# First attention: the last four units of a slot are scaled on ScalarE and added on VectorE

## The chip, the cores and the metric

One core of one Trainium2 chip runs the whole kernel in one launch. The metric is device time in microseconds (us). The kernel before took 5300.93 us, the median of three runs (5298.13 to 5308.7). Five engines work beside each other, each through its own instruction queue in order: TensorE (PE, with its weight loads as PEld), VectorE (DVE), ScalarE (ACT), GpSimd (POOL) and SyncE (SP). They wait for each other through semaphores.

## What is computed

The reference is a graph network of two layers on 6250 nodes with 256 features, each layer an attention over 106250 edges followed by a mixture of experts:

```python
x = x + L0_gnn(layernorm(x), edges)     # attention 0: 4 heads of 64
x = x + L0_ffn(layernorm(x))            # 6 experts, the best 2 of each node
x = x + L1_gnn(layernorm(x), edges)     # attention 1: 1 head of 256
x = x + L1_ffn(layernorm(x))            # 8 experts, all of them, weighted

# attention, per edge (src -> dst) and head
e = leaky_relu(a_src[src] + a_dst[dst])
m = segment_max(e, dst)
e = exp(e - m[dst])
out[n] = sum over edges into n of e * h[src] / sum over edges into n of e
```

The edges come sorted by destination. The change touches attention 0 alone.

## The kernel before, in words

**Tiles, units and slots.** The 6250 nodes are 50 tiles of 125. The edges of a tile are cut into units of 256 (`UE`), 464 units in all, in the order of the tiles, so that some nine units in a row belong to one tile. Eight units (`U`) make a slot, and there are 58 slots. `attention(l, acc, sc)` writes the program of each engine as a function `slot(i, r, t)`. The first and last slots are unrolled, the others are a hardware loop of three slots per turn, with three buffers (`RING`).

**A running maximum.** The softmax is made in one pass. `acc` holds, for each node of each tile, the sum so far of the weighted rows and of the weights: 4 heads x 65 columns (`W`, 64 features and the weight's sum). When a unit raises the maximum, what is in `acc` must be multiplied by a factor first. The factors of a slot are `c1`, made on ScalarE in L867 (an Exp of `delta`). The merge of one unit is `acc = acc * c1 + sum`, with the sum in a PSUM bank, per head because each head has its own factor.

**The stations of a slot i**, by engine:
- SP loads the unit's edge records (`pack`, L658) and its destination rows (`drow`, L671).
- POOL gathers the source rows from HBM into `G` by indirect DMA (L687), 16 for a slot, two per unit. Before the two of unit u it waits until TensorE has summed unit u of slot i - 3, whose rows lie in the buffer.
- TensorE in iteration i: two transposes for slot i - 1 once its rows have landed (L734, L735), the sums of units 4 to 7 of slot i - 3 (L720, with `spread` 0 and 1, L705, ahead of unit 7), two transposes (L746, L747), the sums of units 0 and 1 of slot i - 2, the small product `V` (L757), `spread` 2 and 3, the sums of units 2 and 3, and the product `Xe` (L770). Four banks are shared: unit u and unit u + 4 use the same one, so each sum waits for the merge four units before.
- ScalarE in iteration i: a copy `LT` (L825), then `place` (L791, two operations) and `hit` (L803) for each of four quarters of the slot, the Exp `w` of slot i - 2's weights (L833), a copy `RS_hi` (L840), eight copies `rhsA` (L850), and the factors `c1` (L867).
- VectorE in iteration i: `dloc` (L970), reductions and small operations that end in `te` (L996) and `SEL` (L1001), then the weights are multiplied into `G` in four quarters, `scale(0)` to `scale(3)` (L940, 128x1024 each), with the merges between them, the scan of the maxima (L1014 to L1061, among them `gone`, L1028, which waits for `V`), and the one-hot matrices of slot i, `incidence(0)` to `(3)` (L957).

**The merges' places.** On VectorE `scale(0)`, merges of units 4 and 5 of slot i - 3, L1007, `scale(1)`, merges of units 6 and 7, then the scan; the merges of units 0 to 3 of slot i - 2 stand at the iteration's end, between the `incidence` steps. The function is `merge(k, u)`, and it has two ways:

```python
if u in own:
    v.wait_ge(S(p + "lowered"), scaled_acc(k, i, u))
    ins = nc.vector.tensor_tensor(at, at, sum_bank(u)[0:TN, 0:HW], ALU.add)          # L918
else:
    for h in range(H):
        ins = nc.vector.scalar_tensor_tensor(at, at, c1[...], sum_bank(u)[...], ALU.mult, ALU.add)   # L925
ins.then_inc(S(p + "acc"), 1)
```

`own` holds the units that are not in `FUSED[l]`. In the kernel before it is empty in both layers, so all merges go by L925, and ScalarE's counterpart `lower(k, u)` (from L805 on) returns without an instruction wherever it is called.

Of the kernel before, what the change touches and what calls it, by code (L numbers as in the profile page):

```python
# [36 lines left out]
U = 8  # L37
# [18 lines left out]
assert UE == 1 << LOG_UE and (SU + LAG) % RING == 0 and RING * V % MR == 0 and SU * U <= KU * P and (NG + 1) % 2 == 0 and EP * EC == E  # L56

HEADS = (4, 1)
FUSED = ((0, 1, 2, 3, 4, 5, 6, 7), (0, 1, 2, 3, 4, 5, 6, 7))
SLOPES = (0.2, 0.01)  # L60
EXPERTS = (6, 8)
XT = 256
# [5 lines left out]
def build(nc, a, out):  # L68
    ctx = ExitStack()
    with ctx:  # L70
# [6 lines left out]
        def S(name):  # L77

            if name not in sems:
                sems[name] = nc.alloc_semaphore(name=f"{name}_{stage[0]}")  # L80
            return sems[name]
# [8 lines left out]
        def after(eng, name, count):  # L90

            if not isinstance(count, int) or count > 0:
                eng.wait_ge(S(name), count)
# [53 lines left out]
        def late(i, k):  # L147

            return not isinstance(i, int) or i >= k
# [395 lines left out]
        def attention(l, acc, sc):  # L545
# [9 lines left out]
            K3 = C + 1  # L555
            own = [u for u in range(U) if u not in FUSED[l]]
            NA = len(own)
# [64 lines left out]
            def has(i, lag):  # L622

                return not isinstance(i, int) or lag <= i < SU + lag
# [13 lines left out]
            with nc.Block() as block:  # L638
# [137 lines left out]
                def _(act):  # L776
                    tile_regs = [[act.alloc_register(f"{p}atile{k}_{u}") for u in range(U)] for k in range(RING)]

                    def slot(i, r, t):
# [3 lines left out]
                        def place(v_):  # L783

                            if not one:
                                return
                            act.wait_ge(S(p + "spread"), i * V - V + (v_ + 1))
                            if v_ >= 2 or late(i, 2):
                                after(act, p + "MT", i * V - V + (v_ - 1))
                            for k in range(2):  # L790
                                ins = nc.scalar.activation(mt_d[:, v_ % 2, k * C:(k + 1) * C, :],  # L791
                                                           bank[2 + v_ % 2][0:TN, k * UE:(k + 1) * UE].rearrange("p (e c) -> p c e", c=C), ACT.Abs,
                                                           bias=unode[0:TN, bass.ds(i * U - U + (2 * v_ + k), 1)])
                            ins.then_inc(S(p + "mt_abs"), 1)

                        def hit(v_):

                            if not one:
                                return
                            act.wait_ge(S(p + "mt_abs"), i * V - V + (v_ + 1))  # L800
                            if late(i, 3 if v_ < 2 else 2):
                                after(act, p + "Xe", i - 2 if v_ < 2 else i - 1)
                            nc.scalar.activation(MT[:, turn(r, 1, v_), :, :], mt_d[:, v_ % 2, :, :], ACT.Relu, bias=ones[0:TN, 0:1], scale=-1.0).then_inc(S(p + "MT"), 1)  # L803

                        def lower(k, u):  # L805

                            if u not in own or not has(i, k):
                                return
                            rk = (r - k) % RING
                            j = act.snap(tile_regs[rk][u], min_val=0, max_val=NT - 1)  # L810
                            if u == own[0]:
                                act.wait_ge(S(p + "c1"), i - k + 1)
                            if u or late(i, k + 1):
                                after(act, p + "acc", i * U - k * U + u)
                            for h in range(H):
                                at = acc[:, bass.ds(j * HW + h * W, W)]
                                ins = nc.scalar.activation(at, at, ACT.Copy, scale=c1[:, rk, u, h:h + 1])
                            ins.then_inc(S(p + "lowered"), 1)

                        if one:  # L820
                            act.reg_load(tile_regs[r1], unit_j[0:1, bass.ds(i * U - U, U)])
                            act.wait_ge(S(p + "rowT"), i)
                            if late(i, 2):
                                after(act, p + "SEL", i - 1)
                            nc.scalar.copy(LT[:, :], rowT_ps[:, P:2 * P]).then_inc(S(p + "LT"), 1)  # L825
                        place(0)
                        lower(3, U - 2)
                        hit(0)
                        if two:

                            act.wait_ge(S(p + "te"), i - 1)
                            to = wt[:, r2, :, :] if l == 1 else G[:, r2, :, :].rearrange("p q (h w) -> p q h w", h=H)[:, :, :, DH]
                            nc.scalar.activation(to, te[:, :, :], ACT.Exp).then_inc(S(p + "w"), 1)  # L833
                        lower(3, U - 1)
                        place(1)
                        if one:
                            act.wait_ge(S(p + "selT"), i)
# [4 lines left out]
                        if one:  # L842
# [7 lines left out]
                                ins = nc.scalar.copy(rhs[:, u, :, 0:KT, :].rearrange("p s k h -> p s (k h)"),  # L850
                                                     tab[:, bass.ds(j, 1), :, :, :].rearrange("p o s k h -> p (o s) (k h)"))
                            ins.then_inc(S(p + "ad_in"), 1)
                        lower(2, 0)
                        place(2)
                        lower(2, 1)
                        hit(2)
                        place(3)
                        lower(2, 2)
                        hit(3)
                        lower(2, 3)  # L860
                        lower(2, 4)
                        lower(2, 5)
                        if one:
                            act.wait_ge(S(p + "delta"), i)
                            if late(i, RING + 1):
                                after(act, p + "acc", i * U - U * RING)
                            nc.scalar.activation(c1[:, r1, :, :], delta[:, :, :], ACT.Exp).then_inc(S(p + "c1"), 1)  # L867
                    run(act, slot)

                @block.vector  # L870
# [1074 lines left out]
```

## Time and profile before

| | us |
|---|---|
| median of three runs | 5300.93 |
| the profiled execution | 5292.68 |
| its span, first to last instruction | 5290.9 |
| granted TensorE clock over the span, share of full speed | 0.778 |
| PE busy | 3470.2 (66%) |
| VectorE busy | 2702.5 (51%) |
| POOL busy | 2200.9 (42%) |
| ScalarE busy | 1540.1 (29%) |
| attention 0, from its first factors to its last (L867, 58 of them) | 253.5 to 1647.5 |

The span is 1.8 us shorter than the profiled execution's own time. The busy shares are means over stages with different limits, so the stage that the change touches has to be read by itself. Two labels of the releasers are leftovers: semaphore numbers are used again from stage to stage, and in attention 0 a wait of L791 that is put down to `DMA X<-in_x` is a wait for TensorE's `spread` (L705), and a wait of L825 put down to `DMA ubase<-unit_base` is one for TensorE's transpose L735. The code has no other waits there of that kind.

### The profile page before, as it was taken

How to read it: one execution, taken by the hardware profiler on the slowest of the kernel's cores; microseconds unless marked ns; L12 is line 12 of the kernel's file. 1: busy time of each engine (PE TensorE's matmuls, PEld its weight loads, DVE VectorE, ACT ScalarE, POOL GpSimd, SP SyncE). 2: the span in 40 equal slices, each digit the busy share in tenths (PEclk: the TensorE clock that was granted, in tenths of full speed). 3: DMA queues.
4: the chain of work that ended last, by engine and by line, in shares of the span. 5: the costliest groups of instructions: out<-in, count | busy, mean ns of one | idle time of the engine just before them, and what ended most of it. 6: DMA issues, size and time to landing. Idle time of an engine off the chain costs nothing. (4 is left out here: it accounts for less than half of the span.)

```text
span 5290.9 us, 78218 instructions
## 1 busy us (share of the span) xinstructions
PE 3470.2 (66%) x16240; PEld 2639.6 (50%) x16241; DVE 2702.5 (51%) x8451; ACT 1540.1 (29%) x4325; POOL 2200.9 (42%) x2095
## 2 busy tenths in 40 slices
PE   5166566666656788753545555445555799999999
PEld 3144344444434677632333333333333688888887
DVE  7377777777777855463444444444444531122221
ACT  2133323332322123311222222222222233333333
POOL 0377777777771033285655555555554000000000
PEclk9576777676776589966766666677677899999999
DMA  3233333333344144443333333333335100000000
GB/s 100 72 90 87 87 89 86 89 88 87 89 85 84 33 144 156 130 105 86 83 73 74 71 75 79 71 75 76 73 78 65 51 7 6 6 6 6 6 6 6
DMA packets 382420, 367.81 MB, mean 70 GB/s; under 512 B 249324, under 2 KB 309388, under 8 KB 382242
## 3 DMA queue, kind: packets, MB, share of 16 engines
q0 software_dynamic: 107072, 272.84, 20.9%
q1 hardware_dynamic: 272774, 92.39, 7.3%
q10 hardware_dynamic: 2396, 0.84, 0.1%
q14 instruction: 144, 1.18, 0.1%
q8 instruction: 34, 0.56, 0.0%
HBM read 324.13 MB, written 41.59 MB: 69 GB/s over the span
## 5 line engine op out<-in xcount | busy, mean ns | idle before, releaser
L687 POOL DMA_INDIRECT g_G<-rows,g_pack x1856 | 1946.6, 1049 | 1336.8 <-DMA g_pack<-edge_pack 621.3
L720 PE MATMUL bank<-g_G,g_MB 128*125 128x260 f32 x1856 | 704.3, 542 | 214.6 <-DVE acc L925 86.2
L720 PE MATMUL bank<-g_G,g_M 128*125 128x257 f32 x1856 | 672.0, 524 | 157.4 <-issue 101.2
L791 ACT ACTIVATE g_mt_d<-bank,unode 125x256 bf16<-125x256 f32 x928 | 384.5, 464 | 1196.0 <-DMA n_yg<-expert_out,pos_i 451.9
L925 DVE SCALAR_TENSOR_TENSOR acc<-acc,g_c,bank 125x65 f32 (+1 forms) x2320 | 621.5, 317 | 113.2 <-issue 55.9
L720 PEld LDWEIGHTS bank<-g_G,g_MB 128*125 128x125 f32 x1856 | 473.9, 269 | 401.1 <-issue 172.8
L720 PEld LDWEIGHTS bank<-g_G,g_M 128*125 128x125 f32 x1856 | 470.0, 266 | 312.0 <-issue 177.0
L1365 DVE SCALAR_TENSOR_TENSOR X<-bank,e_cw,X 125x256 f32 (+1 forms) x400 | 175.2, 480 | 845.1 <-PE bank L1191 845.1
L1261 ACT ACTIVATE e_h<-bank,e_bi_c,e_sc_c 128x250 f32<-128x250 f32 x800 | 403.6, 555 | 559.6 <-PE bank L1182 421.6
L770 PE MATMUL bank<-g_rhs,g_MT 125*128 125x24 bf16 (+1 forms) x1856 | 65.3, 171 | 491.1 <-issue 461.7
L1191 PE MATMUL bank<-e_w,e_h 128*125 128x256 f32 x1600 | 377.8, 379 | 3.1 <-ACT e_h L1261 3.1
L1182 PE MATMUL bank<-e_h,e_w 128*128 128x250 f32 x1600 | 378.4, 379 | 1.2 <-ACT e_h L1261 1.2
L1173 PE MATMUL bank<-e_xnT,e_w 128*128 128x250 f32 x1600 | 372.4, 375 | 0.0
L803 ACT ACTIVATE g_MT<-g_mt_d,ones 125x512 bf16<-125x512 bf16 x464 | 335.5, 723 | 14.1
L770 PEld LDWEIGHTS bank<-g_rhs,g_MT 125*128 125x128 bf16 x1856 | 58.1, 100 | 560.5 <-issue 548.0
L940 DVE TENSOR_TENSOR g_G<-g_G 128x1024 f32<-128x1024 f32 x232 | 283.3, 1222 | 97.2 <-ACT g_G L833 74.8
L1191 PEld LDWEIGHTS bank<-e_w,e_h 128*125 128x125 f32 x1600 | 299.1, 187 | 47.3 <-ACT e_h L1261 3.9
L1173 PEld LDWEIGHTS bank<-e_xnT,e_w 128*128 128x128 f32 x1600 | 304.0, 190 | 36.4 <-issue 0.7
L1182 PEld LDWEIGHTS bank<-e_h,e_w 128*128 128x128 f32 x1600 | 297.1, 191 | 43.3 <-issue 8.0
L957 DVE TENSOR_TENSOR g_MB<-iota_b,g_dloc 128x500 f32<-128x500 bf16 (+1 forms) x464 | 302.3, 674 | 0.1
L825 ACT COPY g_LT<-bank 64x128 f32<-64x128 f32 (+1 forms) x116 | 29.7, 256 | 847.7 <-DMA ubase<-unit_base 436.0
L1785 POOL DMA_INDIRECT x_xg<-expert_in,ids x108 | 111.1, 1029 | 298.5 <-PE bank L1801 200.0
(302 smaller groups left out, 4162.1 us busy)
## 6 DMA issues: line engine op xcount, KB each, us to landing
g_G<-rows,g_pack POOLq DMA_INDIRECT x1856
acc<-in_edge_attr SPq DMA_DIRECT2D x50, 531.2 KB
g_pack<-edge_pack SPq DMA_DIRECT2D x928, 2.0 KB
g_drow<-edge_dst SPq DMA_DIRECT2D x928, 1.0 KB
expert_out<-x_y SPq DMA_DIRECT2D x54, 256.0 KB
g_qe<-edge_q SPq DMA_DIRECT2D x464, 1.0 KB
rows<-acc SPq DMA_DIRECT2D x25, 253.9 KB
rows<-n_T SPq DMA_DIRECT2D x25, 251.0 KB
```

Of the source, the lines that this page charges most:

```text
L687: nc.gpsimd.indirect_dma_start(G[:, r, q, :], None, rows_d[l], bass.IndirectOffsetOnAxis(ap=pack[:, r, q, 0:1], axis=0)).then_inc(S(p + f" ...
L720: mm_ = nc.tensor.matmul(sum_bank(u)[0:TN, 0:HW], left, G[:, rk, q, :], start=(c == 0), stop=(c == C - 1))
L791: ins = nc.scalar.activation(mt_d[:, v_ % 2, k * C:(k + 1) * C, :], bank[2 + v_ % 2][0:TN, k * UE:(k + 1) * UE].rearrange("p (e c) -> p c ...
L803: nc.scalar.activation(MT[:, turn(r, 1, v_), :, :], mt_d[:, v_ % 2, :, :], ACT.Relu, bias=ones[0:TN, 0:1], scale=-1.0).then_inc(S(p + "MT" ...
L925: ins = nc.vector.scalar_tensor_tensor(at, at, c1[:, rk, u, h:h + 1], sum_bank(u)[0:TN, h * W:(h + 1) * W], ALU.mult, ALU.add)
L940: ins = nc.vector.tensor_tensor(g[:, :, 0:DH], g[:, :, 0:DH], g[:, :, DH:W].broadcast_to([P, CP * H, DH]), ALU.mult)
L957: nc.vector.tensor_tensor(MB[:, r, at, :], iota_b[:, 0:TN].unsqueeze(1).broadcast_to([P, CP, TN]), dloc[:, r, at, 0:1].broadcast_to([P, CP ...
L1173: mm = nc.tensor.matmul(bank[m][:, 0:GN], w1[:, e, k, m * P:(m + 1) * P], xnT[:, r, k, :], start=(k == 0), stop=(k == 1))
L1182: mm = nc.tensor.matmul(bank[2 + m][:, 0:GN], w2[:, e, k, m * P:(m + 1) * P], h1[:, k, :], start=(k == 0), stop=(k == 1))
L1191: mm = nc.tensor.matmul(bank[4 + u][0:TN, 0:D], h2[:, e % 2, k, u * TN:(u + 1) * TN], w3[:, e, k, :], start=(k == 0), stop=(k == 1))
L1261: ins = nc.scalar.activation((h1 if q == 0 else h2[:, e % 2, :, :])[:, m, :], bank[2 * q + m][:, 0:GN], ACT.Relu, bias=bi_c[:, q, m, e:e + ...
L1365: ins = nc.vector.scalar_tensor_tensor(xt, bank[4 + u][0:TN, 0:D], cw[:, r, u, e:e + 1], xt, ALU.mult, ALU.add)
```

## The change

`FUSED` of layer 0 now holds units 0 to 3 alone, so `own` is units 4 to 7. For each of these 232 units ScalarE multiplies the unit's accumulator by the factors, four activations of 125x65 (`lower`, L817, one per head), and VectorE adds the PSUM sum with one `tensor_tensor` of 125x260 (L918) in place of four operations of 125x65. `lower(3, u)` waits for `c1` of that slot (unit 4 only) and for the merge before (`acc`); `merge` waits for `lowered`. The calls of `lower` get new places in ScalarE's order. Those that are taken out wrote no instruction.

```diff
-FUSED = ((0, 1, 2, 3, 4, 5, 6, 7), (0, 1, 2, 3, 4, 5, 6, 7))
+FUSED = (tuple(range(4)), tuple(range(8)))
...
                             nc.scalar.copy(LT[:, :], rowT_ps[:, P:2 * P]).then_inc(S(p + "LT"), 1)
+                        lower(3, 4)
                         place(0)
-                        lower(3, U - 2)
                         hit(0)
                         if two:
...
                             nc.scalar.activation(to, te[:, :, :], ACT.Exp).then_inc(S(p + "w"), 1)
-                        lower(3, U - 1)
+                        lower(3, 5)
                         place(1)
...
                             ins.then_inc(S(p + "ad_in"), 1)
-                        lower(2, 0)
+                        lower(3, 6)
+                        lower(3, 7)
                         place(2)
-                        lower(2, 1)
                         hit(2)
                         place(3)
-                        lower(2, 2)
                         hit(3)
-                        lower(2, 3)
-                        lower(2, 4)
-                        lower(2, 5)
                         if one:
                             act.wait_ge(S(p + "delta"), i)
```

`lower`, as it stands in the code:

```python
if u == own[0]:
    act.wait_ge(S(p + "c1"), i - k + 1)
if u or late(i, k + 1):
    after(act, p + "acc", i * U - k * U + u)
for h in range(H):
    at = acc[:, bass.ds(j * HW + h * W, W)]
    ins = nc.scalar.activation(at, at, ACT.Copy, scale=c1[:, rk, u, h:h + 1])
ins.then_inc(S(p + "lowered"), 1)
```

VectorE's order is not changed. Attention 1 and the other stages are not touched.

## Rows read from the trace of the kernel before

**Rows 1.** The page: busy tenths of VectorE and POOL, slices of 132 us.
```profile
DVE  7377777777777855463444444444444531122221
...
POOL 0377777777771033285655555555554000000000
```

**Rows 2.** Busy time in attention 0: start, length, engines, clock, DMA.
```profile
300.00:1500.00 1200.00, 737.57 (x3488) 496.49 (x3489) 915.86 (x3151) 364.87 (x1166) 868.93 (x777) 0.71 0.35 88
```

**Rows 3.** Groups of L687, POOL's only line, 300 to 1500 us.
```profile
L687 POOL DMA_INDIRECT g_G<-rows,g_pack x777 | 869.9, 1120 | 331.4 <-issue 215.7 <-remote 61.7 <-PE bank L720 53.4
```

**Rows 4.** Timeline of a long stall: start, us, engine, line, what [idle before].
```profile
603.10 0.74 PE L705 MATMUL bank<-g_drow,ones_bf 2*125 2x512 bf16 x2
...
609.85 0.95 POOL L687 DMA_INDIRECT g_G<-rows,g_pack  x1 [0.30 <-issue]
612.67 0.23 DVE L1028 TENSOR_SCALAR g_gone<-bank 125x64 f32<-125x64 f32 x1 [7.81 <-remote]
612.81 0.84 ACT L791 ACTIVATE g_mt_d<-bank,unode 125x256 bf16<-125x256 f32 x2 [13.66 <-DMA X<-in_x]
...
613.58 0.95 POOL L687 DMA_INDIRECT g_G<-rows,g_pack  x1 [2.78 <-remote]
```

**Rows 5.** Timeline of one ordinary slot, from PE's transposes on.
```profile
1031.61 0.27 PE L735 MATMUL bank<-ident,g_dloc 128*64 128x128 f32 x1
...
1034.76 0.64 PE L705 MATMUL bank<-g_drow,ones_bf 2*125 2x512 bf16 x2
...
1038.69 0.94 POOL L687 DMA_INDIRECT g_G<-rows,g_pack  x1 [0.30 <-issue]
1038.99 0.26 ACT L825 COPY g_LT<-bank 64x128 f32<-64x128 f32 x1 [9.16 <-DMA ubase<-unit_base]
...
1040.84 0.84 ACT L791 ACTIVATE g_mt_d<-bank,unode 125x256 bf16<-125x256 f32 x2 [1.59 <-DMA X<-in_x]
...
1041.30 0.95 POOL L687 DMA_INDIRECT g_G<-rows,g_pack  x1 [1.67 <-remote]
...
1042.34 0.30 ACT L833 ACTIVATE g_G<-g_te 128x64 f32<-128x64 f32 x1
...
1043.81 0.85 DVE L925 SCALAR_TENSOR_TENSOR acc<-acc,g_c,bank 125x65 f32 x4
...
1044.72 3.83 PE L720 MATMUL bank<-g_G,g_MB 128*125 128x260 f32 x8 [3.50 <-issue]
...
1048.04 0.86 DVE L925 SCALAR_TENSOR_TENSOR acc<-acc,g_c,bank 125x65 f32 x4 [0.24 <-DVE acc L925]
...
1049.30 1.22 DVE L940 TENSOR_TENSOR g_G<-g_G 128x1024 f32<-128x1024 f32 x1
1049.39 1.94 POOL L687 DMA_INDIRECT g_G<-rows,g_pack  x1 [0.30 <-issue]
...
1051.49 0.23 DVE L1028 TENSOR_SCALAR g_gone<-bank 125x64 f32<-125x64 f32 x1 [0.97 <-remote]
```

**Rows 6.** Timeline of the slot after it, at its start.
```profile
1061.66 0.86 DVE L925 SCALAR_TENSOR_TENSOR acc<-acc,g_c,bank 125x65 f32 x4 [2.45 <-PE bank L720]
...
1061.89 0.26 ACT L825 COPY g_LT<-bank 64x128 f32<-64x128 f32 x1 [7.07 <-DMA ubase<-unit_base]
1062.27 0.84 ACT L791 ACTIVATE g_mt_d<-bank,unode 125x256 bf16<-125x256 f32 x2
...
1065.25 0.32 ACT L833 ACTIVATE g_G<-g_te 128x64 f32<-128x64 f32 x1 [1.39 <-issue]
```

**Rows 7.** Groups by shape, 150 to 1700 us: busy us, mean ns of one.
```profile
L925 DVE SCALAR_TENSOR_TENSOR acc<-acc,g_c,bank 125x65 f32 x1856 | 399.5, 277 | 66.8 <-issue 38.6 <-DVE acc L925 20.4 <-PE bank L720 7.2
...
L791 ACT ACTIVATE g_mt_d<-bank,unode 125x256 bf16<-125x256 f32 x464 | 192.3, 464 | 472.9 <-DMA X<-in_x 216.9 <-PE bank L705 194.2 <-issue 59.2
L803 ACT ACTIVATE g_MT<-g_mt_d,ones 125x512 bf16<-125x512 bf16 x232 | 168.0, 724 | 7.1
...
L1033 DVE TENSOR_TENSOR g_SB<-g_SB,bank 125x64 f32<-125x64 f32 x58 | 15.4, 266 | 2.0
```

## The prediction, made before the changed kernel ran

> **What bounds the kernel now.** The chain that ended last lies in the dense experts, so it says nothing of attention 0. I went from the slices to the stage. In the first 13 slices VectorE is busy seven tenths of the time and POOL seven to eight [rows 1]; neither is full, so a slot is paced by a chain with waits. In the 1200 us from 300 on POOL issued 777 gathers, 16 a slot, hence 48.6 slots of 24.7 us [rows 2, 3].
>
> POOL's slot: a gather lasts 1.120 us in the mean and the least step to the next is 0.30 us [rows 3, 5], so 16 x 1.42 = 22.7 us. The rest of its idle time is (331.4 - 777 x 0.30) / 48.6 = 2.0 us a slot, one pause. It comes where POOL needs TensorE to have summed unit 4 of the slot three back. That sum is not late in the records: TensorE's L705, which stands behind it in the queue, is recorded as done at 1035.40, yet ScalarE's L791, which waits for L705, starts at 1040.84 and POOL goes on at 1041.30 [rows 5]. POOL's last gather before had ended at 1039.63, 1.2 us before ScalarE's start. The long stall shows the same more plainly: L705 is recorded as done at 603.84, POOL gathers until 610.80, and at 612.67 and 612.81 VectorE and ScalarE start after 7.8 and 13.7 us of nothing [rows 4]. So as I read it, TensorE's signals are held back while POOL issues gathers without a break, and come through one to two us after POOL stops. POOL stops because it needs one of them. The slot is then POOL's 22.7 us plus its pause, and VectorE, ScalarE and TensorE have slack.
>
> **The change, part by part.**
>
> (1) The add. L1033, a two-operand operation with one operand in PSUM, takes 266 ns for 64 columns, and L940 takes 1.22 us for 1024 [rows 5, 7], 1.0 ns a column; 260 columns give 0.46 us. The four L925 took 0.85 [rows 5]. VectorE saves 0.39 x 232 = 90 us of busy time (at least 0.85 - 0.46, at most 0.85 - 0.27 = 0.58 each, were the add as short as L1033). All of it lies beside POOL's work, so it is worth nothing by itself.
>
> (2) The scaling. The nearest rows are L791 with 256 columns, 464 ns and 0.38 apart (two end after 0.84), and L803 with 512 columns, 724 ns [rows 5, 7]: also 1.0 ns a column. An activation of 65 columns is then 0.27 us, one starts 0.19 after the other, and a unit's four take 0.27 + 3 x 0.19 = 0.84 us. Bounds: below, 4 x 65 columns at 1.0 ns, 0.26 us; above, two L791 pairs, 1.7 us. I take 0.84, which is read off the same engine. ScalarE gets 195 us more work and is busy 365 of 1200 us now [rows 2], so load is no matter; order is.
>
> (3) The hand-over. Unit 5 can be scaled only after unit 4 is merged, 6 after 5, 7 after 6. For each step I take the 0.24 us that VectorE needs between two merges [rows 5], and 0.15 for the way back (between nothing and 0.3). Counted from the end of L833 (1042.64): scale(0) to 1.25, merge 4 to 1.65, lower 5 to 2.7. Behind lower 5 on ScalarE wait L791, L840, L803 and the eight L850, which now end about 2.5 us later, at 5.2; lower 6 ends at 6.1, merge 6 at 6.7, lower 7 at 7.75, merge 7 at 8.4. Before, merge 7 ended at 1048.90, which is 6.3. **Plus 2.1 us** for merge 7 and what is queued behind it on VectorE: the scan, scale(2), scale(3), the factors, four merges, the one-hot matrices. At L1028 VectorE waited 0.97 us for a signal of TensorE [rows 5]; that wait is used up first, so the tail is 1.2 us late.
>
> (4) Lower 4 stands between L825 and L791. Where L825 comes early (here 1039.25 against 1040.84 [rows 5]) it is hidden. Where L825 itself was held (1062.15 against 1062.27 [rows 6]) L791, L803, L833 and scale(0) start 0.8 us later. Of the 50 slots in the middle, 25 are of the second kind.
>
> (5) TensorE. Unit 0's sum starts as soon as merge 4 has freed the bank (1044.72 after 1044.66 [rows 5]), so 0.39 us earlier, and unit 1's after it. Unit 2 needs merge 6, at 6.7 against a start at 7.3; unit 3 needs merge 7, at 8.4 against about 9.2. Nothing of it is late.
>
> (6) Is the lateness absorbed? From one L833 to the next it is 22.9 us in the pair of slots shown, with 0.97 + 2.45 us of waits for TensorE in it [rows 5, 6]: 19.5 us of work. The turn of the loop adds about 2 us in one slot of three, mean 20.2. Plus 2.1, plus 0.8 where L825 was held: 23.1, under 24.7. TensorE's unit 4 is summed 4 us before POOL asks, and 1 to 2 us of that go. POOL's pace stays.
>
> (7) What can move POOL: gathers last 0.94 us at least but 1.12 in the mean [rows 3, 5]; the long ones lie under L940, as 1.94 us at 1049.39 under L940 from 1049.30 [rows 5]. A gather that starts under such an operation with both operands in SBUF ends after it. Scale(0) now starts after a gather's start and costs none. Shifted by 0.8 us in 29 slots of 58 it meets the next gather's start, for up to 1.0 us each, 0 to +29 us; scale(1) and (2), shifted too, may lose stretch, some -20. I take +8 us. The skill says otherwise: the Trainium skill's page SBUF — State Buffer, section Who interferes with whom, infers that such an operation doesn't stall the writing of descriptors, since it takes the read side alone; the row of 1.94 us speaks against that, and by the page this term would be 0 and the sum 5300.9. For the new add I take nothing, as its second operand is in PSUM.
>
> **Sum:** the profiled execution 5292.7 + 8 = 5300.7. The median of runs is 8.3 above that execution, so 5309.
>
> **The rivals.**
>
> A, above: POOL's pace holds. Its own range is 5290 to 5335.
>
> B, slower: ScalarE and VectorE handing the accumulator to and fro become the pace. For it: 23.1 us is near 24.7, and waits that are held may not be absorbed. Against: 3.4 us of waits in the pair shown. Its place is lower 5 to merge 7. Each of the four lowers on that chain would have to cost 0.4 us more than 0.84, or signals be held in one more slot of three. At the upper bound, 1.7 us, the slot is 23.1 + 3.4 = 26.5, +1.8 x 58 = +104 us; halfway +50. So 5350 to 5405. The Trainium skill's page ScalarE: Activation LUTs, section Rules for kernel authors, sends multiplications to VectorE; with that page's figures for an activation with a pointer operand my estimate is 1.06 us a unit, which alone would make the chain 24.0 and leave A standing.
>
> C, faster: what paces the slot is merge 4, units 0 and 1, V, L705, and the signals are late by TensorE's own work. Then 0.39 us of each slot goes, less 0.8 in the held half where scale(0) is late: between -23 and 0, so 5278. If VectorE's shorter tail counts as well, 5255. Against: 603.84 to 612.81 [rows 4].
>
> D, slower: the new add stretches gathers as L940 does. A gather's start falls under 0.46 us in 0.46 of 1.42 cases and then costs 0.23 in the mean, +17 us; at most 0.46 x 232 = +107. So 5326.
>
> **How the numbers follow.** About 0.2% (11 us) is what a measurement of this kernel can tell from no change. A has 0.50 (same 0.32, slower 0.13, faster 0.05), B 0.26 (all but 0.01 slower), C 0.18 (0.17 faster), D 0.06 (slower). Faster 0.22, same 0.34, slower 0.44. The forecast is A's 5309. The range takes in most of C and B: 5270 to 5390.
>
> **What would show it.** In the changed profile: L918 232 times at 0.4 to 0.5 us; L817 928 times, four in 0.8 to 1.1 us; VectorE idle before L918 of units 5, 6 and 7, ended by ScalarE; L1028 without its wait; POOL's mean gather 1.10 to 1.16 us and its idle beyond 0.30 still near 2.0 us a slot. B is right if POOL's idle time grows by 0.9 us a slot or more while its gathers stay at 1.12. C is right if that idle shrinks. D is right if gathers are long under L918. I am wrong on the whole if the 58 factors (L867) span less than 1380 us or more than 1420, against 1394 now.

## The result, and the profile after

The changed kernel takes 5351.73 us (median of 6 runs, 5338.78 to 5367.4), the kernel before on the same chip 5304.82 (6 runs, 5278.14 to 5314.89). The ratio is 1.0092, interval [1.0071, 1.0113]: **slower by 47 us**. The time lies in the range (5270 to 5390) but not where the forecast put it (5309): it is in rival B's band, 5350 to 5405.

Where it went, by the first and last start of the factors in each attention (L867, now L863) and by the borders of the stages:

| stage, us | before | after |
|---|---|---|
| attention 0, 58 factors | 1394 | 1444 |
| between the two attentions' gathers | 827 | 820 |
| attention 1, 58 factors | 1610 | 1620 |
| dense experts (their first TensorE instruction) to the end | 1159 | 1157 |

The profiled execution has a span of 5342.2 us, 51.3 more than before, and attention 0 has 50 of it. Only this stage has to be explained. The changed kernel's lines past `merge` are four lower than before: L921 is L925, L936 is L940, L953 is L957, L1024 is L1028; the new add is L914, the scaling L817.

The page of the changed kernel, busy tenths of VectorE and POOL in slices of 134 us, beside [rows 1]:

```profile
DVE  7366666666666865553444444444444532121211
...
POOL 0366666666663023265555555555555000000000
```

Both engines of the stage are less busy than before and nothing is nearer to full. The stretch 300 to 1500 us (start, length, busy time of PE, PE loads, VectorE, ScalarE, POOL, clock, DMA share), beside [rows 2]:

```profile
300.00:1500.00 1200.00, 753.22 (x3348) 476.59 (x3348) 796.43 (x2459) 555.00 (x1871) 793.08 (x749) 0.68 0.34 85
```

VectorE lost 119 us of work (some 34 of them because fewer slots fall into the stretch), ScalarE gained 190, and still there are only 749 gathers where there were 777. The granted clock fell as well, 0.71 to 0.68, but that is not the loss: it falls from 0.74 to 0.69 between f1 and f2 below, whose times are equal. The same stretch, POOL's group (busy us, mean ns of one, idle before and what ended it), beside [rows 3]:

```profile
L687 POOL DMA_INDIRECT g_G<-rows,g_pack x749 | 793.1, 1059 | 406.9 <-issue 203.7 <-PE bank L720 128.2 <-remote 75.0
```

749 / 16 is 46.8 slots of 25.6 us. Two things moved against each other. The gathers became **shorter**, 1.059 us for 1.120, which by itself is worth 16 x 0.061 = 1.0 us a slot. The idle time beyond the least step of 0.30 is (406.9 - 749 x 0.30) / 46.8 = 3.9 us a slot for 2.0. The sum is +0.9 a slot, and 58 slots make some 50 us.

Who waits now is in the groups by shape, 150 to 1700 us, of the changed kernel:

```profile
L817 ACT ACTIVATE acc<-acc,g_c x896 | 245.5, 341 | 275.8 <-DVE acc L914 116.8 <-issue 110.2 <-DVE acc L921 47.6
L921 DVE SCALAR_TENSOR_TENSOR acc<-acc,g_c,bank 125x65 f32 x912 | 195.3, 277 | 20.9 <-DVE acc L921 13.0 <-issue 6.8 <-ACT g_c L863 0.8
L791 ACT ACTIVATE g_mt_d<-bank,unode 125x256 bf16<-125x256 f32 x464 | 191.2, 462 | 267.4 <-DMA X<-in_x 236.9 <-PE bank L705 22.5 <-issue 7.6
...
L914 DVE TENSOR_TENSOR acc<-acc,bank 125x260 f32 x224 | 94.6, 422 | 275.8 <-ACT acc L817 159.1 <-issue 109.8 <-PE bank L720 6.9
...
L825 ACT COPY g_LT<-bank 64x128 f32<-64x128 f32 x58 | 15.0, 258 | 255.4 <-DMA ubase<-unit_base 160.9 <-PE bank L735 80.0 <-issue 14.6
L1024 DVE TENSOR_SCALAR g_gone<-bank 125x64 f32<-125x64 f32 x58 | 12.9, 222 | 115.3 <-remote 113.8 <-PE bank L757 1.4
```

and, of the kernel before, the two groups that [rows 7] leave out:

```profile
L825 ACT COPY g_LT<-bank 64x128 f32<-64x128 f32 x58 | 15.0, 258 | 537.8 <-DMA ubase<-unit_base 436.0 <-PE bank L735 67.7 <-issue 34.1
L1028 DVE TENSOR_SCALAR g_gone<-bank 125x64 f32<-125x64 f32 x58 | 12.9, 222 | 53.9 <-issue 26.7 <-remote 24.7 <-PE bank L757 1.4
```

The adds cost 94.6 us of work but VectorE stands 275.8 us ahead of them, for ScalarE. The view ends before the changed kernel's last merges (896 of 928 scalings, 224 of 232 adds, 912 of 928 fused ones). Up to 1745 us it has 254.1 us of L817, 198.7 + 98.0 = 296.7 us of L921 and L914, and 21.7 + 284.5 = 306.2 us of idle time ahead of these two, where the old merges had 399.5 and 66.8 [rows 7]. So the merges are 103 us less of work and 137 us more of work and waits together (602.9 for 466.3). The other mover is the wait of `gone` for TensorE's `V`, 53.9 to 115.3 us, +1.1 a slot, while ScalarE waits only half as long for the transpose (L825).

One slot of the changed kernel (start us, us, engine, line, what, [idle before and who ended it]):

```profile
987.78 0.42 PE L735 MATMUL bank<-ident,g_dloc 128*64 128x128 f32 x1
...
990.65 0.26 ACT L825 COPY g_LT<-bank 64x128 f32<-64x128 f32 x1 [3.49 <-DMA ubase<-unit_base]
...
991.49 0.94 POOL L687 DMA_INDIRECT g_G<-rows,g_pack  x1 [1.68 <-PE bank L720]
992.45 1.07 ACT L817 ACTIVATE acc<-acc,g_c  x4 [1.54 <-issue]
...
995.42 0.30 ACT L833 ACTIVATE g_G<-g_te 128x64 f32<-128x64 f32 x1
...
996.89 0.42 DVE L914 TENSOR_TENSOR acc<-acc,bank 125x260 f32 x1
997.44 1.07 ACT L817 ACTIVATE acc<-acc,g_c  x4 [1.72 <-DVE acc L914]
998.41 0.81 ACT L791 ACTIVATE g_mt_d<-bank,unode 125x256 bf16<-125x256 f32 x2
998.65 0.43 DVE L914 TENSOR_TENSOR acc<-acc,bank 125x260 f32 x1 [1.34 <-ACT acc L817]
...
1000.78 1.07 ACT L817 ACTIVATE acc<-acc,g_c  x4
1000.92 0.63 PE L757 MATMUL bank<-g_RS,g_MB 128*128 128x12 bf16 x16
1001.99 0.42 DVE L914 TENSOR_TENSOR acc<-acc,bank 125x260 f32 x1 [1.23 <-issue]
1002.54 1.07 ACT L817 ACTIVATE acc<-acc,g_c  x4 [0.69 <-DVE acc L914]
1003.75 0.43 DVE L914 TENSOR_TENSOR acc<-acc,bank 125x260 f32 x1 [1.34 <-issue]
...
1006.92 0.94 POOL L687 DMA_INDIRECT g_G<-rows,g_pack  x1 [0.30 <-issue]
1009.39 0.22 DVE L1024 TENSOR_SCALAR g_gone<-bank 125x64 f32<-125x64 f32 x1 [3.59 <-remote]
1009.53 0.84 ACT L791 ACTIVATE g_mt_d<-bank,unode 125x256 bf16<-125x256 f32 x2 [5.92 <-DMA X<-in_x]
...
1010.30 1.07 POOL L687 DMA_INDIRECT g_G<-rows,g_pack  x1 [2.44 <-remote]
```

Two things are to be seen. The merges climb like a ladder, 1.07 us of scaling and 0.42 of adding in turn; the last ends at 1004.18, 8.46 us after L833. And `V` (L757) is recorded as done at 1001.55, but `gone` starts at 1009.39: VectorE, ready at 1005.80, stands 3.59 us. POOL's last gather ends at 1007.86 and POOL goes on at 1010.30. This is the held signal of [rows 4], now on VectorE's path.

POOL's 3.9 us are two pauses a slot (means of 47 slots). Ahead of unit 2's gathers it now stands 1.97 us where it stood 0.06, and it goes on 4.2 us after the sum that it needs is recorded as done: a held signal, as at 1010.30. Ahead of unit 4's it stands 1.65 us for 1.60, but the kind has changed: before, it went on 7.3 us after the recorded end of that sum, and now 1.0 us after it, as at 991.49. There POOL waits for a sum that is really not there yet. TensorE, for its part, no longer waits for POOL: L734, the transpose that needs the gathered rows, stood idle for them in 25 of 58 slots before (103.7 us), and in 2 now (63.0 us, the first rows of all).

### The profile page after: what moved, and what is told of

It is laid out like the page before. It is cut to its first block and busy times, and to the rows that moved or that the text cites. A ratio compares the mean times of both kernels' runs of the same rounds, so it can differ in the third digit from the quotient of the medians.

```text
span 5342.2 us, 78972 instructions
## 1 busy us (share of the span) xinstructions
PE 3514.4 (66%) x16240; PEld 2633.8 (49%) x16241; DVE 2597.6 (49%) x7755; ACT 1791.4 (34%) x5253; POOL 2136.9 (40%) x2095
## 5 line engine op out<-in xcount | busy, mean ns | idle before, releaser
L687 POOL DMA_INDIRECT g_G<-rows,g_pack x1856 | 1891.2, 1019 | 1447.5 <-DMA g_pack<-edge_pack 640.5
L720 PE MATMUL bank<-g_G,g_MB 128*125 128x260 f32 x1856 | 749.9, 564 | 184.7 <-DVE acc L914 116.4
L791 ACT ACTIVATE g_mt_d<-bank,unode 125x256 bf16<-125x256 f32 x928 | 383.4, 463 | 1048.1 <-DMA n_yg<-expert_out,pos_i 508.7
L921 DVE SCALAR_TENSOR_TENSOR acc<-acc,g_c,bank 125x65 f32 (+1 forms) x1392 | 420.7, 344 | 65.6 <-DVE acc L921 27.5
L817 ACT ACTIVATE acc<-acc,g_c x928 | 254.1, 341 | 294.0 <-DVE acc L914 122.3
L803 ACT ACTIVATE g_MT<-g_mt_d,ones 125x512 bf16<-125x512 bf16 x464 | 335.2, 722 | 12.7
L953 DVE TENSOR_TENSOR g_MB<-iota_b,g_dloc 128x500 f32<-128x500 bf16 (+1 forms) x464 | 302.3, 674 | 0.3
L936 DVE TENSOR_TENSOR g_G<-g_G 128x1024 f32<-128x1024 f32 x232 | 282.6, 1218 | 20.4 <-issue 16.3
L1024 DVE TENSOR_SCALAR g_gone<-bank 125x64 f32<-125x64 f32 (+1 forms) x116 | 23.0, 198 | 496.2 <-remote 492.4
```

What stands on the lines that cost most here:

```text
L687: nc.gpsimd.indirect_dma_start(G[:, r, q, :], None, rows_d[l], bass.IndirectOffsetOnAxis(ap=pack[:, r, q, 0:1], axis=0)).then_inc(S(p + f" ...
L720: mm_ = nc.tensor.matmul(sum_bank(u)[0:TN, 0:HW], left, G[:, rk, q, :], start=(c == 0), stop=(c == C - 1))
L921: ins = nc.vector.scalar_tensor_tensor(at, at, c1[:, rk, u, h:h + 1], sum_bank(u)[0:TN, h * W:(h + 1) * W], ALU.mult, ALU.add)
L936: ins = nc.vector.tensor_tensor(g[:, :, 0:DH], g[:, :, 0:DH], g[:, :, DH:W].broadcast_to([P, CP * H, DH]), ALU.mult)
L953: nc.vector.tensor_tensor(MB[:, r, at, :], iota_b[:, 0:TN].unsqueeze(1).broadcast_to([P, CP, TN]), dloc[:, r, at, 0:1].broadcast_to([P, CP ...
```

## The experiments

Twelve kernels ran, in four groups, each group on one chip beside runs of the kernel before. The chips turned out to be of two kinds. The kernel before takes 4760.12 us (e1 to e4, 11 runs) and 4748.62 (f1 to f4, 19 runs) on two of them, 5383.47 (g1, 17 runs) and 5302.0 (h1 to h3, 18 runs) on the other two; the result above is from a chip of the second kind. Ratios are always against the kernel before on the same chip. Between groups the chips differ, and slots of different groups are compared across chips. "Slot" below is the mean over 47 slots in the middle of attention 0, from one L833 to the next.

### First group (4760 us chip): which part costs

**e1**: ScalarE scales unit 4 alone; **e2**: units 4 and 6.

```diff
-FUSED = (tuple(range(4)), tuple(range(8)))
+FUSED = ((0, 1, 2, 3, 5, 6, 7), tuple(range(8)))     # e1
+FUSED = ((0, 1, 2, 3, 5, 7), tuple(range(8)))        # e2
```

> Only unit 4 is scaled on ScalarE, between L825 and L791; units 5 to 7 are merged as before. One hand-over of four is left, the one that is ready early. Hand-over theory: no wait of VectorE for ScalarE; merge 4 ends 0.43 us earlier, so unit 0's sum too, and L791 starts up to 1.07 us later in the slots where L825 was held. 5270 to 5310, equal to before or a little under. If every group of ScalarE costs its share, a quarter of the loss: 5315.

> Units 4 and 6 are scaled on ScalarE, 5 and 7 merged as before. Each scaling has a fused merge before it, so lower 6 can run while VectorE does L1007 and scale(1). But it stands behind ScalarE's eight copies, which end 2 us before merge 6 in the kernel before, and takes 1.07. Hand-over theory: merge 6 waits for nothing or a few tenths; 5260 to 5310. If every group of ScalarE costs its share, half the loss: 5328.

**e3**: the adds, without any scaling of units 4 to 7 (that factor is left out of the computation); each add waits for the merge before it.

```diff
                             if u in own:
-                                v.wait_ge(S(p + "lowered"), scaled_acc(k, i, u))
+                                if u or late(i, k + 1):
+                                    after(v, p + "acc", i * U - k * U + u)
```

> Left out: the scaling of units 4 to 7 by the factors; VectorE adds their sums in one operation and waits for nobody but the sum and the merge before. Two theories of the 47 us. Hand-over theory: the loss lies in the way from VectorE to ScalarE and back (lower 5, merge 5, ..., merge 7); without it VectorE only gains 0.43 us a unit and the time is at or under that of the kernel before, 5240 to 5300. Add theory (the new operation with one operand in PSUM stretches POOL's gathers, or takes longer than it saves): the loss stays, 5330 or more, with POOL's mean gather above 1.12 us.

**e4**: the hand-over alone. ScalarE waits and signals at the changed kernel's places but multiplies nothing; VectorE waits for that and does the four old operations.

```diff
-                            for h in range(H):
-                                at = acc[:, bass.ds(j * HW + h * W, W)]
-                                ins = nc.scalar.activation(at, at, ACT.Copy, scale=c1[:, rk, u, h:h + 1])
-                            ins.then_inc(S(p + "lowered"), 1)
+                            held(act, p + "lowered")
```

> Same computation as before: VectorE keeps the four operations of 125x65 for units 4 to 7. ScalarE scales nothing, but at the places of the changed kernel it waits for the merge before and signals, and VectorE waits for that signal. Hand-over theory: most of the loss is here too. A step back and forth costs about 0.3 us more than before, and the steps at units 6 and 7 wait for ScalarE's copies, so merge 7 ends 1.5 to 2.5 us later than before: 5325 to 5375. If the loss is ScalarE's work of 1.07 us a unit, or the add, and not the order, the time is that of the kernel before within 10 us.

Measured: e1 4739.36, ratio 0.9954 [0.9939, 0.9968]; **e2 4715.82, 0.9907 [0.9892, 0.9922]**; e3 4810.21, 1.011 [1.0091, 1.0128]; e4 4736.74, 0.9949 [0.993, 0.9968]. Slots: 22.74, 22.38, 22.22, 22.74 us. The expectations were written for a kernel of 5301 us. As ratios, e1 is in its band (0.994 to 1.002), e2 a little under its own (0.992 to 1.002), e3 above its own (0.989 to 1.000), and e4 meets neither of its two (1.004 to 1.014, or within 10 us): it is 23 us faster. POOL's groups of e2 and e3, 300 to 1400 us:

```profile
L687 POOL DMA_INDIRECT g_G<-rows,g_pack x786 | 861.3, 1096 | 239.5 <-issue 217.0 <-PE bank L720 22.5
```

```profile
L687 POOL DMA_INDIRECT g_G<-rows,g_pack x793 | 859.2, 1083 | 241.7 <-issue 219.2 <-PE bank L720 22.5
```

Both have 0.30 us between gathers and next to nothing more: 16 x (1.096 + 0.30) = 22.3, 16 x (1.083 + 0.30) = 22.1. So on this chip the slot is POOL's 16 gathers. Scaling one or two units on ScalarE leaves POOL the pace, and the stage gets shorter because the gathers do (1.118 and 1.096 us in e1 and e2, 1.146 in f1 below). e3 is slower as a whole although its attention 0 is the shortest of the four: its gathers span 1287 us there, but 1293 in attention 1, whose code is the same and which takes 1193 to 1194 in e1, e2 and e4. The granted clock of e3 (first line) lies below that of e1 on the same chip (second line; the kernel before has the same digits on the next group's chip) in slices 22 to 29, where attention 1 runs; from 2300 to 3500 us it is 0.73 against 0.81:

```profile
PEclk9677777777777579977677777777778999999999
```

```profile
PEclk9677777777777559996678888888878999999999
```

What reaches attention 1 are other numbers than in the other kernels, since a factor is left out. Whether that moves the clock was not tried. For attention 0 e3 is clear, for the whole kernel it is not to be used.

What was missing in this group was the changed kernel itself on such a chip.

### Second group (4749 us chip): the same pair again, and two probes

**f1** is the kernel before, **f2** the changed kernel, unaltered. **f3** is the changed kernel, and POOL waits for `V` before the gathers of unit 7, so that its pause falls where the signal is needed:

```diff
+                            if l == 0 and u == 7 and (not isinstance(i, int) or i >= 1):
+                                pool.wait_ge(S(p + "V"), i)
```

> The kernel before, for its trace on the chip of these runs. In the trace of the prediction TensorE's transpose L735 is recorded done 7.2 us in the mean before ScalarE's L825 starts; in the traces of the first four experiments it is 0.5 us and POOL never pauses. If the chip makes the difference, this trace shows either the one or the other through the whole of attention 0 and 1; if the kernels did, this one shows 7 us wherever it runs.

> The changed kernel beside the kernel before. Hand-over theory: where TensorE's signals are held back, 1.006 to 1.012 of the kernel before as measured; where they aren't, POOL alone paces the slot, its idle time is 0.30 us a gather in both kernels, and the change is worth only what it does to the mean gather: 0.995 to 1.005. If the hand-over costs by itself, it is slower by 0.5% or more on any chip.

> The changed kernel, but POOL waits for TensorE's product V of the same iteration before the gathers of unit 7. Holding theory (signals come through when POOL stops): where signals are held, L1024 (gone) no longer waits for V and L705's signal comes at once; POOL pauses 1 to 2 us here and no longer at unit 2 of the next slot; 5290 to 5350 if the kernel before is near 5300. Where signals are not held: POOL's stop costs what V is later than POOL, 0 to 2 us a slot, 0 to +100 us against the changed kernel, and nothing is gained.

**f4** is the kernel before with every second gather of attention 0 left out from slot 3 on; the rows that are then summed are those gathered in the first slots.

```diff
                             for q in range(u * C, (u + 1) * C):
+                                if l == 0 and q % 2 == 1 and (not isinstance(i, int) or i >= RING):
+                                    continue
```

> Kernel before with half the gathers of attention 0 left out from slot 3 on (the second 128 rows of each unit keep old data, so the sums are of other rows). POOL's work falls from 22.7 to 11.4 us a slot. If POOL's pace bounds the slot, it becomes 19.5 to 21 us, VectorE's own chain, and attention 0 is 150 to 250 us shorter than before where signals are held, 100 to 180 where not. If TensorE's signals are late by TensorE's own work, the slot stays at 24 us or more where they are held.

Measured: f1 4749.53 (one run), **f2 4748.13, ratio 0.9995 [0.9986, 1.0005]**, f3 4749.79, 1.0005 [0.9996, 1.0015], f4 4593.45 (one run). f2, f3 and f4 are in their bands. On this kind of chip the change does nothing. First f1 (POOL's group of 300 to 1400 us, then two groups of 150 to 1700):

```profile
L687 POOL DMA_INDIRECT g_G<-rows,g_pack x759 | 869.5, 1146 | 231.3 <-issue 201.1 <-PE bank L720 30.2
```

```profile
L825 ACT COPY g_LT<-bank 64x128 f32<-64x128 f32 x58 | 15.0, 258 | 407.1 <-PE bank L735 407.1
L1028 DVE TENSOR_SCALAR g_gone<-bank 125x64 f32<-125x64 f32 x58 | 12.6, 218 | 1.4 <-PE bank L757 1.4
```

and f1's timeline around a transpose:

```profile
620.65 0.42 PE L735 MATMUL bank<-ident,g_dloc 128*64 128x128 f32 x1
...
621.10 0.26 ACT L825 COPY g_LT<-bank 64x128 f32<-64x128 f32 x1 [4.77 <-PE bank L735]
```

L825 starts 0.03 us after L735's end; the mean of 47 slots is 0.06. In the profile before it is 6.8 in the mean, and 7.1 in the slot shown in [rows 5]. `gone` never waits (1.4 us in 58 slots). Here signals are prompt, POOL gathers without a pause beyond 0.30 us, and the slot is 16 x (1.146 + 0.30) = 23.1 us, measured 23.19. It is the same program: what differs is when TensorE's signals are seen.

f2, the changed kernel on this chip, same views:

```profile
L687 POOL DMA_INDIRECT g_G<-rows,g_pack x762 | 803.6, 1055 | 297.7 <-issue 209.2 <-PE bank L720 88.5
```

```profile
L914 DVE TENSOR_TENSOR acc<-acc,bank 125x260 f32 x232 | 98.0, 422 | 234.4 <-ACT acc L817 199.0 <-PE bank L720 35.4
...
L1024 DVE TENSOR_SCALAR g_gone<-bank 125x64 f32<-125x64 f32 x58 | 12.5, 215 | 1.5 <-PE bank L757 1.5
```

The gathers are 0.091 us shorter, so POOL alone would need 16 x (1.055 + 0.30) = 21.7; but it now pauses (297.7 - 762 x 0.30) / 47.6 = 1.5 us a slot, for TensorE's sums, and the slot is 23.25. f2's expectation of 0.30 us a gather in both kernels fails here. The pause is not a held signal: `gone` waits for nothing, and POOL goes on 1.0 us after the recorded end of unit 4's sum, the one that it waits for. It is the chain through VectorE and ScalarE. TensorE's L734 says the same: in f1 it stands idle for gathered rows in all 58 slots (328.7 us), in f2 in 5 (86.7 us, nearly all in the first slots). From L833's end to the end of merge 7 it has 8.54 us where f1 has 6.26, and VectorE's `te` is ready 0.55 us before L833 starts where f1 has 2.95 to spare. So the 2.3 us that the hand-over costs are paid out of that slack to its end, and the chain takes POOL's place as the pace at the same length.

f3 moved nothing: with prompt signals there is nothing to release. f4's slot is 20.50 us, with 416 gathers in 1100 us; that is the length of the old VectorE and ScalarE chain when POOL does not pace it, 20.2 in the prediction's step (6). With f2's +2.28 it is 22.8, and the changed kernel has 23.25.

### Third group (5383 us chip): another choice of units

**g1**: units 0, 4 and 6 on ScalarE, with unit 0's scaling after `hit(2)`; no two such units follow each other.

```diff
-FUSED = (tuple(range(4)), tuple(range(8)))
+FUSED = ((1, 2, 3, 5, 7), tuple(range(8)))
...
                         hit(2)
+                        lower(2, 0)
```

> Units 0, 4 and 6 are scaled on ScalarE, each behind a merge in one step on VectorE, unit 0 between L803 and L791 of the third and fourth quarter. No scaling waits for another. On a chip where TensorE's signals come at once POOL paces the slot (22.3 us with units 4 and 6): VectorE's saving of a further 0.43 us a slot is beside it, 0.988 to 0.995 of before. If signals are held here, VectorE's chain is 1.3 us shorter than before: 0.975 to 0.992.

Measured 5376.65, ratio 0.9994 [0.9967, 1.0022], a miss: the signals are held here, and 0.975 to 0.992 was expected. POOL's group of 300 to 1500 us and `gone`'s of 150 to 1700:

```profile
L687 POOL DMA_INDIRECT g_G<-rows,g_pack x767 | 831.5, 1084 | 369.9 <-issue 208.0 <-PE bank L720 98.9 <-remote 63.0
```

```profile
L1025 DVE TENSOR_SCALAR g_gone<-bank 125x64 f32<-125x64 f32 x58 | 13.0, 224 | 188.8 <-remote 187.4 <-PE bank L757 1.5
```

Its merge 7 ends 6.06 us after L833, earlier than the old kernel's 6.39, and its gathers are shorter, yet nothing is gained: `gone` waits 3.0 us a slot. (Its slot is 25.08, on a chip on which the kernel before takes 5383 and left no trace, so only the ratio compares like with like.) A shorter chain alone does not help where signals are held; VectorE reaches the wait sooner and stands there. That spoke for holding, and for trying to take it away.

### Fourth group (5302 us chip): the holding itself

**h1** is f4 (half of attention 0's gathers left out) on a chip of the kind with held signals; **h2** is f3, **h3** is e4 there.

> The kernel before with half of attention 0's gathers left out from slot 3 on, again, for a chip on which the kernel before takes 5300 and not 4750. Holding theory: TensorE's signals are held while POOL gathers, so with POOL idle half of the time L825 starts within 1 us of L735 (7.2 before), L791 within 1 us of L705, and attention 0's slot is the same 20.5 us as on the other chips, while attention 1, untouched, keeps its 1.6 ms. If the chip's TensorE signals are late by themselves, the lag stays at some us and the slot at 23 us or more.

> The changed kernel with POOL waiting for V ahead of unit 7's gathers. Holding theory, if this chip is of the 5300 kind: L1024 starts within 1 us of scale(2)'s end, the recorded end of L705 (third quarter) to L791 falls from 5.7 to about 1.5 us, 0.985 to 1.00 of before where the changed kernel had 1.009. If stopping POOL releases nothing, 1.01 to 1.04. On a chip of the 4750 kind 1.000 as before.

> Hand-over without ScalarE's scaling, VectorE's four operations kept, again, for the other kind of chip. Where signals are held and the hand-over is the loss, 1.004 to 1.015; on a chip of the 4750 kind 0.995 as before. If it is under 1.002 where signals are held, the loss of the changed kernel lies in ScalarE's 1.07 us a unit and not in the order.

**h1**: 5054.61 us (one run). h1's lines are up to six higher: L735 is L741, L825 is L831. Its timeline around a transpose:

```profile
611.24 0.27 PE L741 MATMUL bank<-ident,g_dloc 128*64 128x128 f32 x1
611.55 0.26 ACT L831 COPY g_LT<-bank 64x128 f32<-64x128 f32 x1 [1.26 <-PE bank L741]
```

The wait beyond L741's end is 0.04 us here, 0.31 in the mean and 0.11 in the median, where the full kernel has 6.8. The slot is 20.48 us, and that of f4 on the other kind of chip 20.50. All three expectations are met. And attention 1 of the same run, whose gathers are all there, still spans 1619 us, against 1187 in f4. So this chip takes longer than the other kind only while POOL gathers with hardly a break, and it is then that TensorE's signals are seen late. h1 leaves out POOL's instructions and their transfers together; which of the two holds the signals it does not show.

**h2**: 5353.01 us, ratio 1.0102 [1.0068, 1.0137], a miss: 0.985 to 1.00 was expected, and it is as far above the kernel before as the changed kernel is. h2's groups of 150 to 1700 us (lines two higher than the changed kernel's):

```profile
L923 DVE SCALAR_TENSOR_TENSOR acc<-acc,g_c,bank 125x65 f32 x909 | 202.6, 277 | 110.0 <-issue 88.4 <-DVE acc L923 17.1 <-DMA n_att<-in_L_gnn_att_dst 3.4
...
L827 ACT COPY g_LT<-bank 64x128 f32<-64x128 f32 x58 | 15.0, 259 | 527.0 <-DMA unit_i<-unit_table 456.7 <-PE bank L737 70.3
L1026 DVE TENSOR_SCALAR g_gone<-bank 125x64 f32<-125x64 f32 x58 | 12.6, 217 | 15.1 <-DMA edge_dst<-hl 15.1
```

The local part came as expected: the wait at `gone` is gone, 15.1 us for 115.3, and from L705 of the third quarter to L791 it is 1.50 us for 5.72. But 89 us came in ahead of the merges of units 0 to 3 (L923, 110.0 for 20.9), and L827 waits 527.0 again for 255.4. The pause for `V` was no release for the rest of the slot: as I read it, a hold is not attached to one signal, it falls on whatever is waited for while POOL gathers. The slot is 25.79.

**h3**: 5304.3 us, ratio 1.0002 [0.9973, 1.0031], also a miss: 1.004 to 1.015 was expected. It is under 1.002, the expectation's other branch. The waits and the order of the changed kernel without the scaling's time cost nothing measurable. Its merge 7 ends 7.00 us after L833, 0.6 later than in the kernel before, and its slot is 24.81 (in a profiled execution of 5321.93, 18 above its median). So what loses is not the order and not the signalling by themselves. h2, with the whole change in it, loses 1.0% on this same chip; what it has beyond h3, besides POOL's wait, is ScalarE's 1.07 us on each scaling between two merges, and the adds. The adds alone were not run on a chip of this kind. They are shorter than what they replace and stretch no gather (see rival D below), which leaves the 1.07 us.

## Why the prediction was right or wrong

All slots in one table. "POOL" is 16 x (mean gather + 0.30), "rest" is what is left of the slot, "merge 7" is from L833's end to the end of merge 7, "gone" the wait between `scale(2)` and `gone`, "spare" from the end of `te` to L833's start; all us, means of 47 slots, the gather's from 300 us to 1400 or 1500.

| kernel | signals | slot | gather | POOL | rest | merge 7 | gone | spare |
|---|---|---|---|---|---|---|---|---|
| f1 (before) | prompt | 23.19 | 1.146 | 23.1 | 0.1 | 6.26 | 0 | 2.95 |
| f2 (changed) | prompt | 23.25 | 1.055 | 21.7 | 1.6 | 8.54 | 0 | 0.55 |
| e4 (hand-over) | prompt | 22.74 | 1.118 | 22.7 | 0.1 | 6.82 | 0 | 1.91 |
| before | held | 24.67 | 1.120 | 22.7 | 2.0 | 6.39 | 0.49 | 1.84 |
| after | held | 25.59 | 1.059 | 21.7 | 3.9 | 9.35 | 1.57 | 0.50 |
| h3 (hand-over) | held | 24.81 | 1.102 | 22.4 | 2.4 | 7.00 | 1.45 | 0.96 |
| g1 (0, 4, 6) | held | 25.08 | 1.084 | 22.1 | 2.9 | 6.06 | 3.04 | 0.97 |
| h2 (POOL waits for V) | held | 25.79 | 1.048 | 21.6 | 4.2 | 8.74 | 0 | 0.40 |

The forecast was 5309, rival A; 5351.73 lies in the stated range because that took in rival B. A's mechanism, that POOL's pace holds, failed, and so did its own range (5290 to 5335). That the time lies in the stated range is owed to B's condition coming true, not to the mechanism that was forecast.

**What bounds the kernel: right in the main.** POOL's 22.7 us plus a pause in which it waits for a signal that is held. h1 and f1 show the holding that the prediction read out of [rows 4]. But POOL was less firmly the pace than taken: its rows came last for TensorE's transposes in 25 of 58 slots, in f1 in all.

**(1) The add: right.** 422 ns against 0.46 us.

**(2) The scaling: too small.** 1.07 us for a unit's four, against 0.84. One of 65 columns takes 341 ns where L791 and L803, carried on at 1.0 ns a column, gave 0.27 us: the short operation is not on their line. All 232 take 254 us, not 195. The figures of the Trainium skill's page ScalarE: Activation LUTs, section What ACT_TABLE_LOAD costs, gave an estimate of 1.06 in the prediction, and this trace agrees with it for this operation.

**(3) The hand-over: right.** Merge 7 was to end 8.4 us after L833. It is 8.46 in the slot shown, 8.54 in f2, and 8.63 in the changed kernel's median. Part of it is luck. The larger scaling did no harm to the first half, because lower 6 stands behind the eight L850 either way; in the second half its 0.23 us more is offset by the way to ScalarE and back, 0.13 + 0.14 us in the slot shown where 0.24 + 0.15 was taken, and by the shorter add. The mean is 9.35, and the 0.7 above the median are held signals at merges, which the prediction did not have.

**(4), (5): half right.** The sums of units 0 to 3 came in time for POOL: f2, with prompt signals, has no pause ahead of their gathers. Unit 4's did not, see (6). And the place of lower 4 counts: the spare time before L833 went from 1.84 to 0.50.

**(6) "Is the lateness absorbed": this is the step that failed.** The arithmetic was close. It gave a chain of 23.1 us, and the prompt chip shows it at 23.25 in f2. The comparison was wrong: 23.1 was set against the slot of 24.7, as if the 1.6 us between were free. But the slot of 24.7 holds the same signals back for as long as POOL gathers, and a chain that is near 23 us has to take them in itself. Before, the holds fell on ScalarE's L825 (6.8 us after the transpose) and on VectorE in places where 2 to 4 us were to spare. Now L825 waits 2.3, `gone` +1.08, and the merges 0.7 more than in their median. From before to after the slot's parts change by +2.96 (merge 7), -0.03 (`scale(2)`), +1.08 (`gone`), -0.40 (to the last one-hot matrix), -1.52 (to the next `te`) and -1.18 (from there to the next L833, 1.66 to 0.48): the slot's +0.9. The first and third grew by 4.0 us and the others could give up 3.1. On the prompt chip merge 7 is 2.28 later, the spare time 2.40 less, nothing else is held, and the time stays. The step's other sentence failed too: "TensorE's unit 4 is summed 4 us before POOL asks, and 1 to 2 us of that go". The sum was recorded as done 7.3 us before POOL went on, and 1.0 us before it now, on both kinds of chip (7.2 and 1.0 in f1 and f2), so POOL asks before it is there.

**(7) The gathers: wrong sign.** +8 us was taken, the range had some -20. The gathers' time above 0.945 us, counted from the start of each against VectorE's operations in 48 slots, is 2.10 us a slot under L940 before and 1.03 after (2.34 and 0.85 in f1 and f2); 16 x (1.120 - 1.059) = 1.0 us a slot is 57 us of POOL time gained. It bought nothing, for POOL was not what the slot waited for any more. That the long ones lie under L940 holds in every run. About as many start under it (194 in 48 slots before, 181 after), but later, 0.80 us after its start in the mean where it was 0.56 (0.88 and 0.50 in f2 and f1), so less of it is left; which part of the changed order moves them was not tried.

**The rivals.** B was right on its place (lower 5 to merge 7) and its sign, and on the size of +50 us, though not by its price: it asked for 0.4 us more in each lower *or* held signals in one more slot of three. The lowers cost 0.23 more; that the held signals did the rest is what f2 says, where nothing is held and nothing is lost. Its second condition, idle time of POOL up by 0.9 us a slot or more "while its gathers stay at 1.12", was half met: +1.9, with gathers at 1.059. C and D are out: POOL's idle time grew instead of shrinking, and the gathers that start under an add are 0.001 us longer than the shortest in the mean, in the changed kernel and in f2 (with the adds alone, e3, the mean of all is 1.083). "Wrong on the whole if the 58 factors span more than 1420 us" is met: 1444. The chance of 0.26 for B was too low; as I see it mainly because slack was counted in the means of a system whose waits move.

**What stays open.** Why some chips show TensorE's signals late while POOL gathers, and others not, and whether it is POOL's issuing or its transfers that hold them. How the held time divides itself among the waiting engines: h2 shows that it moves, and h3 and g1 that no single length of the chain gives the slot. Why attention 1 is longer in e3. The changed kernel itself was not run again beside h1 to h3. And e2, which is better than both kernels where signals are prompt (ratio 0.9907, where the changed kernel has 0.9995 on the next group's chip), was not run where they are held; its nearest relative there, g1, is even with the kernel before. A version that wins on both kinds was not found.

## What to carry to other kernels

- When work is split between two engines that pass the same tile to and fro, price the ladder (here 1.07 + 0.42 us and about 0.27 for two hand-overs, three times over) and set it against the slack of a run in which nothing else is late; engine load says nothing (VectorE had 103 us less of merging to do, and the kernel takes 47 us more). Small doses with other work between the steps (units 4 and 6) gained 0.9% on the one chip on which they ran, one with prompt signals.
- Slack that is made of waits for late signals is not slack: the waits move to the next place. A chain needs room for its own length and for the lateness, together.

## What was not expected of the hardware

- The same kernel takes 4749 to 4760 us on two chips and 5302 to 5383 on two others (beside the 5301 and 5305 of the first runs). The dense experts take 1156 to 1159 us on all of them; the gathers of attention 0 span 1339 us (f1) for 1433, those of attention 1 1191 for 1636.
- All of it goes with one thing: copies that wait for a recorded transpose start 0.06 us after it on the one kind, 6.8 on the other, and 0.31 on that other kind when half of the gathers are left out.
- A gather of 128 rows takes 0.95 us, but up to 2.0 when it starts under VectorE's 1.22 us product of two SBUF operands; these delays sum to 0.8 to 2.4 us a slot, which seems to hang on how the two engines' rhythms fall. Gathers that start under neither that product nor the one-hot matrices' operations (0.2 to 0.5 us of delay each) are delayed by less than 0.02 us in the mean, with the new adds (whose second operand is in PSUM) and without.
